# A rebuilt prologue for a fused attention and feed-forward kernel: one power per norm, the norm's weight behind the transposes, the residual later, and matmuls of constants ahead of the loads

## What is computed

```
u = layernorm(x)                        # (x - mean) / sqrt(var + 1e-5)
h = u * rsqrt(mean(u*u) + 1e-5) * ln_weight
q, k, v = h @ w_q.T, ctx @ w_k.T, ctx @ w_v.T      # 32 heads of 128
p = softmax(q @ k.T + position_bias, masked)       # per head and batch
x = x + u + (p @ v) @ w_out.T                      # block 1
x = x + low-rank-expert FFN(layernorm(x))          # block 2
x = x + single-head attention(layernorm(x), ctx)   # block 3
x = x + dequantized FFN(layernorm(x))              # block 4
```

## Time and profile before

| | |
|---|---|
| median of 3 runs | 1020.16 us (1019.74 to 1022.96) |
| span of the profiled execution, first to last instruction | 1021.1 us |
| TensorE matmul busy | 992.2 us, 97% |
| VectorE, ScalarE, GpSimd busy | 45%, 37%, 31% |
| TensorE's place in the chain that ended last | 92% of the span |

### The profile page before, as it was taken

One profiled execution on the slowest core, in us unless ns is written; L12 is line 12 of the kernel. 1 busy time (PEld: TensorE's weight loads), 2 busy tenths in 40 slices (PEclk: granted clock), 3 DMA queues, 4 the chain that ended last, 5 costly groups with the idle time before them and its releaser, 6 DMA issues.

```text
span 1021.1 us, 15605 instructions
## 1 busy us (share of the span) xinstructions
PE 992.2 (97%) x5780; PEld 859.8 (84%) x5780; DVE 456.6 (45%) x932; ACT 382.0 (37%) x1025; POOL 317.0 (31%) x283
## 2 busy tenths in 40 slices
PE   6899999999999999999999999999999999999995
PEld 5688888888888888888888888888888888787773
DVE  6743343333333333333333333333333338376764
ACT  5433333333333333333333333333333324324452
POOL 4732222222222222222222222222222220033675
PEclk9899999999999999999999999999999999999999
DMA  8121111111010102020101011111110110211001
GB/s 288 55 81 42 47 42 48 42 43 37 27 49 21 67 21 67 21 67 21 67 21 66 21 46 41 46 41 46 41 46 22 42 42 32 69 77 31 22 22 42
DMA packets 18022, 50.17 MB, mean 49 GB/s; under 512 B 2099, under 2 KB 4275, under 8 KB 17604
## 3 DMA queue, kind: packets, MB, share of 16 engines
q1 hardware_dynamic: 17988, 49.72, 14.2%
HBM read 47.62 MB, written 2.10 MB: 49 GB/s over the span
## 4 chain that ended last, share of the span: by engine, by line
PE 92%; DVE 5%; POOL 1%; DMA 1%; issue 1%; ACT 1%; SPq 0%; POOLq 0%; DVEq 0%; ACTq 0%
PE ps_q L287 7%; PE ps_q L289 7%; PE ps_q L288 7%; PE ps_o L287 6%; PE ps_o L289 6%; PE ps_o L288 6%; PE ps_v L287 6%; PE ps_v L288 6%; PE ps_v L289 6%; PE ps_k L287 6%; PE ps_k L289 6%; PE ps_k L288 6%; PE ps_pv L1292 6%; PE ps_s L1273 6%; PE ps_t L1281 3%; PE ps_q L1471 1%
## 5 line engine op out<-in xcount | busy, mean ns | idle before, releaser
L888 DVE TENSOR_TENSOR att_lo<-ps_pv,att_hi 128x512 fp32r<-128x512 f32 x64 | 44.3, 692 | 404.2 <-ACT att_hi L458 404.2
L465 ACT ACTIVATE probs<-scores,neg_max 128x128 f32<-128x128 f32 x256 | 99.8, 391 | 146.1 <-DVE neg_max L916 146.1
L287 PE MATMUL ps_v<-wv_hi,ct_hi 128*128 128x256 f32 x504 | 147.9, 293 | 1.9 <-DVE wv_lo L857 1.9
L289 PE MATMUL ps_v<-wv_hi,ct_lo 128*128 128x256 f32 x504 | 142.9, 284 | 0.0
L288 PE MATMUL ps_v<-wv_lo,ct_hi 128*128 128x256 f32 x504 | 142.8, 283 | 0.0
L398 ACT COPY kt<-ps_k 128x512 f32<-128x512 f32 x63 | 37.0, 587 | 246.7 <-PE ps_k L289 246.7
L650 POOL TENSOR_TENSOR wq_lo<-raw_q,wq_hi 128x512 fp32r<-128x512 f32 x30 | 38.8, 1295 | 270.5 <-ACT wq_hi L381 270.5
L287 PE MATMUL ps_q<-xt_hi,wq_hi 128*128 128x512 f32 x252 | 105.7, 420 | 0.1
L287 PE MATMUL ps_k<-ct_hi,wk_hi 128*128 128x512 f32 x252 | 99.1, 393 | 6.4 <-DVE ct_lo L800 6.4
L289 PE MATMUL ps_q<-xt_hi,wq_lo 128*128 128x512 f32 x252 | 99.9, 396 | 0.0
L287 PE MATMUL ps_o<-wo_hi,att_hi 128*128 128x512 f32 x256 | 99.8, 390 | 0.0
(11 more groups left out here) (279 smaller groups left out, 1920.2 us busy)
## 6 DMA issues: line engine op xcount, KB each, us to landing
raw_v<-in_w_v SPq DMA_DIRECT2D x16, 512.0 KB, 3.2
raw_q<-in_w_q SPq DMA_DIRECT2D x16, 512.0 KB, 3.2
raw_o<-in_w_o SPq DMA_DIRECT2D x16, 512.0 KB, 3.2
raw_k<-in_w_k SPq DMA_DIRECT2D x15, 512.0 KB, 4.4
acc<-in_x SPq DMA_DIRECT2D x2, 1024.0 KB, 10.3
bias_sb<-in_bias SPq DMA_DIRECT2D x16, 128.0 KB, 3.4
ctx_sb<-in_ctx_nat SPq DMA_DIRECT2D x1, 2048.0 KB, 9.6
out_x<-acc SPq DMA_DIRECT2D x8, 256.0 KB, 2.0
```

The lines of the kernel that those rows point to most:

```text
L287: pe.matmul(dst, hi_l, hi_r, start=first, stop=False)
L289: return pe.matmul(dst, lo_l, hi_r, start=False, stop=last)
L465: e = act.activation(probs[n][:, m, :], scores[n][:, m, :], ACT.Exp, bias=neg_max[:, n, m:m + 1], accum_out=row_sum[:, n, m:m + 1])
L888: dve.tensor_tensor(att_lo[:], blocks(ps_pv), att_hi[:].bitcast(F32), ALU.subtract).then_inc(att_lo_s, 1)
```

## The change

The prologue is rearranged on all five engines; from step 4 on, the programs are the same.

- Norm: layernorm followed by RMS norm has the scale 1/sqrt(var*(1+eps) + eps*eps). VectorE makes that argument (`rms_var`), GpSimd takes one power of it (`h_scale`) and one product (`h_shift`), and ScalarE makes the tile in one activation. `x_mean_square`, `x_scale_rms` and `x_tile` go.
- The weight: ln_weight comes as four rows of 128 (2 KB), is transposed once on TensorE to a column per chunk (`ln_col`), and multiplies when the transposed h leaves PSUM: `x_high` becomes a multiplication, `x_rest` a fused multiply and subtract. The transposes of four tiles now fill the four banks by chunk, so xt_hi and xt_lo come in four pieces per half.
- Order on TensorE: 11 matmuls of `ones` by `ones` first, two more after K(1); all four tiles of the first half are transposed between K(2) and K(3); those of the second half in step 0. V(2) stands ahead of Q(2) in step 0, V(3) moves from step 1 to step 0, and step 1's output product is split around its transposes.
- Residual: x*(1+rstd) - mean*rstd by one activation on ScalarE per tile, two in each of steps 0 to 3 (`x_residual`); a second power on GpSimd makes rstd (`x_scale_residual`). The eight adds on GpSimd go.
- Loads: w_v goes ahead of x, w_q comes in two halves ahead of x's second half, ln_weight shrinks from 256 KB to 2 KB.
- split_o and split_v move from the prologue into ScalarE's step 0; GpSimd's rest_v moves behind the first make_shift of step 0.

The core of the diff, one engine after the other in this order: SyncE, ScalarE, GpSimd, VectorE, TensorE (indentation cut):

```diff
     sp.dma_start(raw_k[:, 1].rearrange("p c d -> p (c d)"), w_k[0, :, D:2 * D]).then_inc(wk_in, 16)
+    sp.dma_start(raw_v[:].rearrange("p c d -> p (c d)"), w_v[0]).then_inc(wv_in, 16)
+    sp.dma_start(ln_rows[:], ln_w.rearrange("o (c p) -> (o c) p", p=P)).then_inc(ln_in, 16)
     sp.dma_start(acc[:, 0:4, :], halves(x)[:, 0:4, :]).then_inc(x_in[0], 16)
-    sp.dma_start(raw_v[:].rearrange("p c d -> p (c d)"), w_v[0]).then_inc(wv_in, 16)
+    sp.dma_start(raw_q[:, 0].rearrange("p c d -> p (c d)"), w_q[0, :, 0:D]).then_inc(wq0_in, 16)
     sp.dma_start(raw_ct[1][:], ctx_t[:, :, HALF:TOK]).then_inc(ct_in[NC], 16)
-    sp.dma_start(ln_w_rows[:], ln_w.broadcast_to([P, D])).then_inc(ln_in, 16)
-    sp.dma_start(acc[:, 4:8, :], halves(x)[:, 4:8, :]).then_inc(x_in[1], 16)
-    sp.dma_start(raw_q[:].rearrange("p h c d -> p (h c d)"), w_q[0]).then_inc(wq_in, 16)
+    sp.dma_start(raw_q[:, 1].rearrange("p c d -> p (c d)"), w_q[0, :, D:2 * D]).then_inc(wq_in, 16)
     sp.dma_start(mask_raw[:], mask).then_inc(mask_in, 16)
     sp.dma_start(bias_sb[:, 0], bias[0]).then_inc(bias_in[0], 16)
+    sp.dma_start(acc[:, 4:8, :], halves(x)[:, 4:8, :]).then_inc(x_in[1], 16)
...
+    def x_high(half, m):
+        act.wait_ge(x_t, 4 * half + 4)
+        if half == 0 and m == 0:
+            act.wait_ge(ln_out, 1)
+        act.mul(xt_hi[:, m, half * HALF:(half + 1) * HALF], x_banks[m][:],
+                ln_col[:, m:m + 1]).then_inc(x_hi, 1)
     def x_norm(b):
+        act.wait_ge(x_shift_s, b // 4 + 1)
+        if b > 3:
+            act.wait_ge(x_t, b - 3)
+        act.activation(h_tile(b), acc[:, b, :], ACT.Identity, bias=h_shift[:, b:b + 1],
+                       scale=h_scale[:, b:b + 1]).then_inc(x_h, 1)
+    def x_residual(b):
+        act.wait_ge(x_res_s, 2 * (b // 4) + 2)
+        act.wait_ge(x_h, b + 1)
+        act.activation(acc[:, b, :], acc[:, b, :], ACT.Identity, bias=nmr[:, b:b + 1],
+                       scale=rstd_one[:, b:b + 1]).then_inc(x_resid, 1)
...
     k_evac(0, 0, 0)
     split_v(0, 0)
     k_evac(1, 0, 1, ps_q)
+    act.wait_ge(wq0_in, 16)
+    act.copy(wq_hi[:, 0], raw_q[:, 0]).then_inc(wq_hi_s, 1)
     for c in range(NC):
         split_ct(1, c)
+    for b in range(4):
+        x_norm(b)
+    k_evac(2, 1, 0)
+    for m in range(NC):
+        x_high(0, m)
     act.wait_ge(wq_in, 16)
     act.copy(wq_hi[:, 1], raw_q[:, 1]).then_inc(wq_hi_s, 1)
+    k_evac(3, 1, 1, ps_q)
+    q_evac(0, 0, 0, ps_k)
+    q_evac(1, 0, 1)
+    for b in range(4, BATCH):
+        x_norm(b)
+    for m in range(NC):
+        x_high(1, m)
...
         exponentials(s, n)
+        if isinstance(i, int) and i == 0 and c == 0:
+            act.wait_ge(ct_lo_done, NC)
+            split_o(0, 0)
...
         pt_evac(s)
+        if isinstance(i, int) and i == 0 and c < 4:
+            x_residual(2 * c)
+            x_residual(2 * c + 1)
+        if isinstance(i, int) and i == 0 and c == 0:
+            act.wait_ge(ct_lo_done, 2 * NC)
+            split_v(1, 1)
...
     def x_scale(half):
         cols = slice(4 * half, 4 * half + 4)
+        pool.wait_ge(x_var, half + 1)
+        pool.tensor_tensor(h_scale[:, cols], rms_var[:, cols], minus_half[:, 0:4], ALU.pow).then_inc(x_pow, 1)
+        pool.wait_ge(x_neg, half + 1)
+        pool.wait_ge(x_pow, 2 * half + 1)
+        pool.tensor_tensor(h_shift[:, cols], neg_mean[:, cols], h_scale[:, cols], ALU.mult).then_inc(x_shift_s, 1)
...
+    rest_q(0)
     x_scale(0)
+    x_scale_residual(0)
     rest_q(1)
     pool.wait_ge(mask_done, 1)
     pool.wait_ge(bias_in[0], 16)
     make_shift(0, 0)
-    for b in range(5, BATCH):
-        x_residual(b)
+    x_scale(1)
+    x_scale_residual(1)
     rest_o(0, 0)
-    rest_v(1, 1)
...
             make_shift(s + 1, (c + 1) % LOOP_STEPS)
+        if isinstance(i, int) and i == 0 and c == 0:
+            rest_v(1, 1)
...
+        dve.tensor_scalar(rms_var[:, cols], mean_var[:, cols, 1], 1.0 + EPS, EPS * EPS, ALU.mult,
+                          ALU.add).then_inc(x_var, 1)
...
+    def x_rest(half, m):
+        dve.wait_ge(x_hi, NC * half + m + 1)
+        cols = slice(half * HALF, (half + 1) * HALF)
+        dve.scalar_tensor_tensor(xt_lo[:, m, cols], x_banks[m][:], ln_col[:, m:m + 1],
+                                 xt_hi[:, m, cols].bitcast(F32), ALU.mult, ALU.subtract).then_inc(x_lo, 1)
...
+    dve.wait_ge(ln_t, 1)
+    dve.tensor_copy(ln_col[:], ps_t[:, 0:NC]).then_inc(ln_out, 1)
+    x_statistics(0, range(4))
+    x_moments(0)
+    v_evac(0, 0, 0)
     for c in range(NC):
         ct_rest(1, c)
     v_evac(1, 0, 1, ps_s)
     dve.wait_ge(mask_in, 16)
     dve.tensor_scalar(mask_sb[:], mask_raw[:], 1.0, MASKED, ALU.subtract, ALU.mult).then_inc(mask_done, 1)
+    x_statistics(1, range(4, 6))
+    dve.wait_ge(ln_out, 1)
+    for m in range(NC):
+        x_rest(0, m)
+    x_statistics(1, range(6, 8))
+    x_moments(1)
...
+        if start:
+            for m in range(NC):
+                x_rest(1, m)
+        elif isinstance(i, int) and s == 1:
+            v_evac(3, 1, 1)
+        elif not drain and not (isinstance(i, int) and s == 2):
             v_evac(s + 1, ((c + 1) // 2) % 2, (c + 1) % 2)
...
+        if start:
+            v_evac(2, 1, 0)
+        else:
             add_output(s - 1, (c - 1) % LOOP_STEPS)
...
+    def warm(count):
+        for _ in range(count):
+            pe.matmul(warm_bank[:, 0:P], ones[:], ones[:], start=True, stop=True)
+    def x_transpose(half):
+        for b in range(4 * half, 4 * half + 4):
+            pe.wait_ge(x_h, b + 1)
+            for m in range(NC):
+                if half == 1 and b == 4:
+                    pe.wait_ge(x_lo, m + 1)
+                last = pe.transpose(x_banks[m][:, b % 4 * P:(b % 4 + 1) * P],
+                                    h_tile(b)[:, m * P:(m + 1) * P], ident[:])
+            last.then_inc(x_t, 1)
+    pe.wait_ge(const_done, 2)
+    warm(11)
     pe.wait_ge(wk_lo_s, 1)
     project_k(0, 0, first_use=True)
     pe.wait_ge(wk_lo_s, 2)
     project_k(1, 1, bank=ps_q)
+    pe.wait_ge(ident_done, 1)
+    pe.wait_ge(ln_in, 16)
+    pe.transpose(ps_t[:, 0:NC], ln_rows[:], ident[0:NC, 0:NC]).then_inc(ln_t, 1)
+    warm(2)
...
     project_v(1, 1, bank=ps_s)
     pe.wait_ge(k_out, 1)
     project_k(2, 2, first_use=True)
+    pe.wait_ge(ln_out, 1)
+    x_transpose(0)
+    pe.wait_ge(k_out, 2)
+    project_k(3, 3, bank=ps_q)
+    pe.wait_ge(wq_lo_s, 1)
     pe.wait_ge(k_out, 3)
+    project_q(0, 0, bank=ps_k, first_use=True)
     pe.wait_ge(wq_lo_s, 2)
     pe.wait_ge(k_out, 4)
+    project_q(1, 1)
...
         step_scores(s, c)
+        if first:
+            x_transpose(1)
+            pe.wait_ge(v_out, t)
+            project_v(t, tc)
         pe.wait_ge(wq_lo_s, 2 * gt + c % 2 + 1)
         pe.wait_ge(q_out, t)
+        project_q(t, tc, first_use=first)
+        if first:
+            step_transpose(s, c)
+            pe.wait_ge(v_out, 3)
+            project_v(3, 3)
+            step_values(s, c)
+            return
+        if isinstance(i, int) and s == 1:
+            output(0, 0, 0, (0,))
+            step_transpose(s, c)
+            output(0, 0, None, (1,))
+            step_values(s, c)
+            return
```

More of the change, by code:

```diff
@@ L124, in build @@
         nmr, _ = place("nmr", [P, BATCH], F32)
[L125 to L128, removed]
+        rms_var, _ = place("rms_var", [P, BATCH], F32)
+        h_scale, _ = place("h_scale", [P, BATCH], F32)
+        h_shift, _ = place("h_shift", [P, BATCH], F32)
+        rstd_one, _ = place("rstd_one", [P, BATCH], F32)
+        ln_col, _ = place("ln_col", [P, NC], F32)
+        ln_rows, _ = place("ln_rows", [NC, P], F32)
         minus_half, _ = place("minus_half", [P, BATCH], F32)
@@ L163, in build, with h_tile @@
         mask_raw, _ = place("mask_raw", [P, BATCH, P], U8, at=at_scores[0])
-        ln_w_rows, _ = place("ln_w_rows", [P, D], F32, at=at_att_hi)
-        rms_in = [place(f"rms_in{n}", [P, D], F32, at=(*at_probs, at_scores[1])[n])[0] for n in range(3)]
+        h_last, _ = place("h_last", [P, D], F32, at=at_probs[1])
+        def h_tile(b):
+            return normed[:, b % 4, :] if b % 4 < 3 else h_last[:]
         wk1_raw, _ = place("wk1_raw", [P, NC, D], F32, at=at_raw)
@@ L217, in build @@
         x_banks = (*ps_o, ps_pv, ps_t)
+        warm_bank = ps_s
         g_banks = (ps_q, ps_k, ps_v, ps_t, ps_pv, ps_o[1], ps_pv, ps_o[1])
@@ L801, in ct_rest, with x_statistics, x_moments @@
                                   ALU.subtract).then_inc(ct_lo_done, 1)
-            def x_statistics(half):
+            def x_statistics(half, tiles):
                 dve.wait_ge(x_in[half], 16)
-                tiles = range(4 * half, 4 * half + 4)
                 for b in tiles:
                     dve.bn_stats(stats[:, b, :], acc[:, b, :]).then_inc(x_stats, 1)
-                for b in tiles:
+            def x_moments(half):
+                for b in range(4 * half, 4 * half + 4):
                     dve.wait_ge(x_stats, b + 1)
@@ L916, in step @@
```

(42 more changed lines are left out.)

139 lines of the change are left out of this document (18 added, 121 removed).

## The result

| | before | changed |
|---|---|---|
| median, first comparison | 1020.28 us (1019.74 to 1022.96, 4 runs) | 1012.14 us (1009.88 to 1012.38, 4 runs) |
| span of the profiled execution | 1021.1 us | 1010.3 us |
| scores of step 2 start at | 66.42 us | 55.12 us |

The ratio is 0.9903, 95% interval [0.9883, 0.9923]: faster by 1.0%. Two more comparisons on other chips gave 0.9896 [0.9876, 0.9915] and 0.9910 [0.9890, 0.9930]. The forecast was 1011.0 us, the range 1008.0 to 1015.2.

The account below looks back on a forecast made before the run. TensorE, busy 925.84 of 930 us from 70 us on, was taken as the bound, so gains must come earlier: 10.0 - 0.8 = 9.2 us off the 1021.1 span, then 0.9 to the median, 1011.0 us; range 1008.0 to 1015.2.

Parts of the forecast that it names:

- Start: First K blocks: ones matmuls raise the clock before K(0), which then waits on its loads; saves 0 to 1.8 us, 1.3 taken.
- rival 1: At the start, the ones matmuls don't raise the clock before K(0): 1.2 us lost, 1012.2 us; chance 8%.
- V and the loads: Prologue: w_v lands at 9.9 us, V(0) starts at 13.3 instead of 15.9; the 1.9 us hole and its slow stretch go.
- Norm of the first half: Prologue: four ScalarE activations end at 21.2 us, ahead of the transposes at 22.0; no holes there, scores(0) at 32.7.
- Step 0: Norms of tiles 4 to 7 make TensorE wait 1.0 us in pieces; no wait for probabilities; scores(1) at 46.7.
- Step 1: neg_max takes 1.25 us beside GpSimd, so TensorE waits 2.6 us for probabilities at the transposes; scores(2) at 56.4.
- Clock in the new holes: Holes of 0.8, 1.0 and 2.6 us might slow the clock; one slow stretch costs 1.7 to 2.5 us; 0.8 taken.
- Rivals 2 and 5: 2: three slow-clock stretches in the holes, 1015.5 us or so, chance 8%. 5: slower, chance 3%.
- Steps 2 and 3: Two residuals per step, 1.5 us of ScalarE, stay hidden behind 3.8 us of TensorE's V block and values.
- rival 3: Steps 1 to 4: residuals make ScalarE late, each output waits for att_lo; up to 4 us, 1015 us; chance 7%.
- Sum: 10.0 us gained at scores(2), less 0.8 for the clock: 9.2; span 1011.9, less 0.9 to the median: 1011.0.
- After it TensorE is full: Behind the scores of step 2 TensorE was full before and stays full, so the front's gain lasts to the end.

Follow-up runs that it names:

- e1_no_warm: The changed kernel without the 11 matmuls of ones ahead of K(0): median 1013.13 us, 1.0 above the changed kernel beside it.
- e0_again: The changed kernel run a second time with no edit: median 1012.13 us (5 runs) beside 1022.61.
- b2_v_first: The kernel before with only the load of w_v moved ahead of x's first half: median 1021.71 us, ratio 1.0002.
- b3_v_and_order: The kernel before with w_v loaded ahead of x's first half and VectorE's half of wv_lo ahead of x's statistics: median 1020.16 us, ratio 0.9997.
- e4_two_powers: The changed kernel with the residual's power and its two small ops ahead of h_scale on GpSimd for x's first half: median 1011.19 us, ratio 0.9899.
- e7_thin_residual: e3_k4_early with x's residual made for only 8 of 512 columns, so its output is incomplete: median 1009.84 us of 2 runs.
- e3_k4_early: The changed kernel with the K block of unit 4 moved from step 2 into step 1, ahead of the transposes: median 1009.68 us (5 runs).
- e0_third: The changed kernel run a third time with no edit: median 1011.95 us (6 runs) beside 1020.16.
- e5_half_k4: The changed kernel with half of unit 4's K block in step 1 and half left in step 2: median 1010.03 us, ratio 0.9889.
- e8_half_k4_again: e5_half_k4 run once more, on the same chip as the changed kernel: median 1009.59 us (6 runs) beside 1011.95.
- b0_again: The kernel before run once more for a second trace: median 1021.08 us (12 runs) against 1020.73 for the same kernel beside it.

## Why the prediction was right, and where it wasn't

- **Start.** Forecast were K(0) at the full clock and V(0) at 13.3: V(0) measured 13.44 and 13.37, in a third execution 15.06. In the first trace the full clock came at K(0)'s third matmul, in the second ahead of K(0). The term, 1.3 us, measured 1.1 with and without the ones (e1_no_warm). The lower bound, 0, was met in e0_again, the upper, 1.8, in no trace; rival 1 came true in one of three executions of the same code. The ones took 5.06 us and ended at 6.19, not at 5.7, still ahead of K(0) at 6.28.
- **V and the loads.** The time was right, the reason half. I gave the whole gain to the load. The earlier trace rows names VectorE's `wv_lo` as what V(0) waited for, and I had read it as w_v being late; b2_v_first shows that in the kernel before the load alone gains nothing. Both were needed, and in the kernel before, with its long norm, even the two together gain nothing (b3_v_and_order).
- **Norm of the first half.** No wait at the transposes, scores(0) at 32.7: 32.79. Of what was removed, the second power weighed at most 0.1 us (e4_two_powers), as I had it beside the path. How the rest divides between the shorter norm and the new order isn't shown. (The 0.83 us ahead of scores(0) come to 0.81 from the rows named.)
- **Step 0.** Scores(1) start at 45.9: 45.92. x_high was 0.6 us apart as taken.
- **Step 1.** This term was mis-sized. I forecast a hole of 2.6 us because `neg_max` would wait for GpSimd. It didn't (VectorE's row, then two of GpSimd's):

```profile
48.95 0.17 DVE L899 TENSOR_SCALAR neg_max<-row_max 128x4 f32<-128x4 f32 x1
```

```profile
47.76 1.30 POOL L667 TENSOR_TENSOR wq_lo<-raw_q,wq_hi 128x512 fp32r<-128x512 f32 x1
49.02 1.30 POOL L670 TENSOR_TENSOR wk_lo<-raw_k,wk_hi 128x512 fp32r<-128x512 f32 x1
```

  It came as one GpSimd instruction ended, and cost 0.17 us, not 1.25; the hole was 1.24 us and scores(2) came 1.3 us earlier than I had them. Whether such an instruction of VectorE meets one of GpSimd at its start or its end is here a matter of 0.4 us: in e7_thin_residual, where GpSimd's two are 0.4 us earlier and this one isn't, it took 1.01 (VectorE's row, then GpSimd's second).

```profile
48.93 1.01 DVE L899 TENSOR_SCALAR neg_max<-row_max 128x4 f32<-128x4 f32 x1
```

```profile
48.61 1.31 POOL L670 TENSOR_TENSOR wk_lo<-raw_k,wk_hi 128x512 fp32r<-128x512 f32 x1
```

  My walk was off by 0.45 us at that point (49.4 against 48.95), so it couldn't decide this; I should have kept both outcomes. In step 2 the same instruction took 0.81 us.
- **Clock in the new holes.** 0.8 us taken, 0 measured: no granted clock under 1.00 between 21 and 60 us in any trace of the changed kernel or its variants. Rivals 2 and 5 didn't happen. (Rival 2's 1010.2 + 5.5 is 1015.7.)
- **Steps 2 and 3.** The residuals are hidden behind K(4) and V(4), as forecast; e7_thin_residual shows that the cover is needed. With K(4) gone from step 2, 0.67 us of rival 3's kind came true (e3_k4_early), far from its 4 us.
- **Sum.** The walk gave 10.0 us at scores(2) against the first trace, and 9.2 with the term for the clock; measured were 11.3, less 0.5 us lost behind it, 10.8 in the span. The medians differ by 8.1, 10.5 and 8.2 us in the three comparisons. What failed is how I went from the profiled execution to the median. All later traces have 1.8 to 1.9 us around the span (1012.16 and 1010.3), so the first trace of before was its execution of 1022.96, 2.8 us above the median, not 0.9. It had one slow stretch more than the other trace of that kernel; I counted its removal, 2.5 us, in full, and then took the 0.9 us off once more. That put the forecast 2.8 us too low. Against it stood 1.3 us too little at step 1 and 0.8 us for a clock that didn't fall, less the 0.5 us behind scores(2): 1.6 us too high. The difference, 1.2 us, is that of 1011.0 against 1012.1. So the account of the front was right in most stages, but that the total came so near is partly luck. Against the other trace of before, the front gives 6.4 + 2.2 = 8.6 us.
- **After it TensorE is full.** True until about 990 us. From scores(2) to the end the traces of the changed kernel and its variants took 953.1 to 956.5 us with the same work. One place where they differ is a slow stretch between 871 and 881 us. The mean granted clock from 868 to 884 us was 1.00 in e4_two_powers, 0.89 in e0_third and e1_no_warm and 0.79 in e0_again, with 953.1, 954.6 and 954.7, and 956.5 us behind scores(2). One kernel, traced in e5_half_k4 with 0.89 and in e8_half_k4_again with 1.00, took 953.5 and 951.9. So one such stretch goes with about 1.6 us. The first trace of the changed kernel, 955.2 us, has 0.89 there and 0.76 in its last 20.6 us. Why the clock falls there in some executions and not in others is open.

## What to carry to other kernels

Walk the order of TensorE with block lengths from the trace: from V(0) on it landed within 0.15 us for 30 us and failed where a short VectorE instruction meets the long ones of GpSimd. When an instruction waits for two producers, follow the one that the waits view names back through its own queue before crediting a load; the fix may be that queue's order, and it may pay only together with the next thing in line. Before a sum is taken from a profiled execution, find which of the timed runs it is. And where one execution differs from the next by more than the edit is worth, compare distances between two landmarks in the traces, not spans.

## What the runs showed of the hardware

- **The moment at which the clock rises is the execution's, not the kernel's.** The same 11 matmuls of ones from 1.1 us on were followed by the full clock by 4.8 us in three traces, at 6.8 to 7.2 us in three, in between in two, and at 10.5 us in e0_again. In e0_again TensorE had worked without a gap from 1.12 to 6.19 us, as long as in the first trace, and then stood 0.77 us, which may be why the rise came later, but nothing here separates that from chance.
- **Nor does a given hole make it fall.** A wait of 1.89 us ahead of V(0) was followed by a slow stretch, one of 1.88 us at the same place in b2_v_first was not, nor one of 1.51 us in b0_again; there two waits of 0.71 and 0.96 us at 22 and 24 us were. The Trainium skill (TensorE: Matmul & The Clock Gate, What's actually happening) says that the default state is throttled and activity releases it; the rows fit that, and they show that a rule by the length of the hole alone doesn't.
- **A short VectorE instruction can last as long as the GpSimd instruction that it meets.** `neg_max`, 128x4 elements, took 0.17 us where no GpSimd instruction was running or the running one had at most 0.12 us to go. Elsewhere it ended within 0.03 us of the end of the one running: after 1.25 us in the kernel before, 1.01 in e7_thin_residual, 0.81 in step 2 of the changed kernel. Other VectorE instructions beside GpSimd, such as the maximum just ahead of it, kept their 0.69 us.
- **ScalarE's multiplication by a per-row column from PSUM** took 0.69 us (L417), and started every 0.57 us where several stood back to back. The plain copy took 0.59. The norm, with scale and bias by row, started every 0.71 us.
